# The gated product of a quantised feed-forward block takes its own maximum, and its scale is made before the up projection's

## The reference, cut to what matters

```
def act_qdq(x):
    scale = max(max|x| / 32767, 1e-12)          # one scale for the whole tensor
    return clip(round(x / scale), -32768, 32767) * scale
x    = act_qdq(layernorm(x))
up   = act_qdq(x @ w_up.T)                      # 4096 x 768
gate = act_qdq(x @ w_gate.T)
sig  = round(sigmoid(gate) * 65536) / 65536     # clipped to 65535
gate = act_qdq(gate * sig)
o    = act_qdq(gate * up)
y    = o @ w_down.T
```

## Time and profile before

| | us |
|---|---|
| median of 3 runs (lowest to highest) | 992.13 (990.31 to 997.55) |
| the profiled execution | 989.66 |
| its span in the trace | 987.9 |

### The profile page before, as it was taken

How to read it: one execution, slowest core, us unless ns; L and a number is a source line. 1 busy time by engine, 2 the same in 40 slices (tenths; PEclk the granted TensorE clock), 3 DMA queues, 4 the chain that set the end, 5 groups by cost and what they waited for, 6 DMA issues and landing times.

```text
span 987.9 us, 13059 instructions
## 1 busy us (share of the span) xinstructions
PE 844.3 (85%) x4557; PEld 542.5 (55%) x4559; DVE 680.4 (69%) x1237; ACT 539.2 (55%) x1009; POOL 307.1 (31%) x236
## 2 busy tenths in 40 slices
PE   4999999699999999888998989799998993008998
PEld 3776666578677887344444445344443441005887
DVE  2566777866765677679889999735425999896333
ACT  2444434555234666677667776134329995983342
POOL 2100000566211123588868887200001431000000
PEclk9999999799999999899899999899998997558999
DMA  8800000010000000000000000000002437710111
GB/s 287 267 1 1 1 1 1 0 55 0 2 12 1 1 1 2 1 1 1 1 1 1 2 2 1 0 1 0 1 0 93 163 149 283 263 71 11 54 54 54
DMA packets 23447, 45.43 MB, mean 46 GB/s; under 512 B 2323, under 2 KB 18646, under 8 KB 22230
## 3 DMA queue, kind: packets, MB, share of 16 engines
q1 hardware_dynamic: 21776, 43.08, 12.2%
q10 hardware_dynamic: 1606, 1.52, 0.5%
HBM read 27.80 MB, written 16.78 MB: 45 GB/s over the span
## 4 chain that ended last, share of the span: by engine, by line
PE 62%; DVE 20%; POOL 7%; ACT 5%; issue 4%; DMA 1%; ACTq 1%; DVEq 0%; POOLq 0%
PE pair L1336 8%; PE pair L1290 8%; PE pair L968 5%; PE pair L1206 5%; POOL hat L597 4%; PE pair L1221 3%; PE pair L1076 3%; PE pair L1103 3%; PE pair L972 3%; DVE peak L1784 3%; PE pair L1182 2%; DVE wide L1779 2%; DVE wide L1807 2%; PE pair L1013 2%; DVE peak L1769 2%
## 5 line engine op out<-in xcount | busy, mean ns | idle before, releaser
L597 POOL TENSOR_TENSOR hat<-hat 128x1024 f32<-128x1024 f32 x62 | 145.5, 2362 | 38.2 <-DVE hat L1645 38.1
L1315 PE MATMUL pair<-xqs,wuT 128*128 128x512 f32 x192 | 85.5, 607 | 4.8 <-ACT up_stage L862 4.8
L1290 PE MATMUL pair<-xqs,wgT 128*128 128x512 f32 x192 | 84.3, 596 | 0.0
L1336 PE MATMUL pair<-wdT,hid 128*128 128x256 f32 x384 | 83.1, 379 | 0.4 <-DVE hid L1826 0.4
L1336 PEld LDWEIGHTS pair<-wdT,hid 128*128 128x128 f32 x384 | 72.9, 190 | 11.1 <-DVE hid L1826 1.2
L514 POOL TENSOR_TENSOR rstd<-lnt,half 128x8 f32<-128x8 f32 (+2 forms) x15 | 26.5, 1767 | 168.0 <-DVE lnt L1380 168.0
L1190 PE MATMUL pair<-rows,sel 32*128 32x512 bf16 x256 | 68.3, 396 | 9.9 <-ACT down_a L817 2.9
L1206 PE MATMUL pair<-hat,vz 128*32 128x128 f32 x1056 | 71.6, 282 | 2.8 <-DVE hat L1645 1.6
L1206 PEld LDWEIGHTS pair<-hat,vz 128*32 128x32 f32 x1056 | 53.8, 112 | 25.7 <-issue 23.4
L1315 PEld LDWEIGHTS pair<-xqs,wuT 128*128 128x128 f32 x192 | 37.2, 195 | 52.5 <-issue 52.0
L968 PE MATMUL pair<-wT,ft_sb 128*128 128x256 f32 x256 | 64.6, 396 | 0.0
(11 more groups left out here) (214 smaller groups left out, 1920.7 us busy)
## 6 DMA issues: line engine op xcount, KB each, us to landing
up_far<-up_stage SPq DMA_DIRECT2D x24, 512.0 KB, 2.6
ups<-up_far SPq DMA_DIRECT2D x8, 1536.0 KB, 6.9
x_sb<-in_x_dram SPq DMA_DIRECT2D x8, 512.0 KB, 7.6
c_sb<-in_ctx_dram SPq DMA_DIRECT2D x8, 512.0 KB, 8.6
out_dram<-x_sb SPq DMA_DIRECT2D x16, 256.0 KB, 2.1
four<-in_c_four_dram SPq DMA_DIRECT2D x1, 1280.0 KB, 5.6
deq<-in_L_ffn_w_gate_dram SPq DMA_DIRECT2D x1, 768.0 KB, 7.1
deq<-in_L_ffn_w_up_dram SPq DMA_DIRECT2D x1, 768.0 KB, 8.8
```

Source lines behind the costliest of these rows:

```text
L597: nc.gpsimd.tensor_tensor(hat[:, n % RING, :], hat[:, (n - 2) % RING, :], hat[:, n % RING, :], ALU.add).then_inc(summed, 1)
L1290: last = mm(bank[2 + oc][:], wgT[:, c, oc * 128:(oc + 1) * 128], xqs[:, s, c, :], start=(c == 0), stop=(c == DC - 1))
L1315: last = mm(bank[2 + oc], wuT[:, c, oc * 128:(oc + 1) * 128], xqs[:, t % 2, c, :], start=(c == 0), stop=(c == DC - 1))
L1336: last = mm(bank[s][:, 0:D], hid[:, s, ic, :], wdT[:, ic, :], start=(ic == 0), stop=(ic == IC - 1))
```

## The change

- `gated(h)` becomes one `tensor_tensor_reduce`: it writes the product times -1 into `wide` and the row maximum of what it writes to a column of `peak`. That covers the negative side of the product. `peak_gated` is gone, and the factor that rounds the product (`unit[:, 3, 3:4]`) is made negative, so that the sign comes back.
- The positive side comes from the gate's signed maximum. `peak_gate` takes a maximum and a minimum for each of the first seven quads in place of one absolute maximum; for the last quad the absolute maximum stays ahead of unit 1 and a signed maximum follows behind it. ACT takes the one value per partition through rounding, sigmoid and rounding (`top_sigmoid`, after half 4), DVE multiplies it (`top_product`, at half 8).
- `whole_sigmoid` of the even halves goes from ACT to DVE, h % 4 = 1 from DVE to POOL, h % 4 = 3 from POOL to DVE.
- Units 2 and 3 change places. PE's `spread_peak(2)` stands ahead of the last up pair and serves unit 3. The last three up pairs are copied by ACT behind the last sigmoid; DVE takes two of their maxima between the steps of unit 3, and the third behind it.
- ACT rounds two halves of the gated product ahead of unit 2, and then alternates `whole_up(h)` and `whole_g2(h + 2)`.
- `g2q` takes the first place in the shared memory, `ups` follows; quad t uses slot 1, 0, 2 in turn. SP fetches the first quad of `up_far` once the last gated product is done, ahead of the stores of the last three pairs.

```
@@ -406,7 +408,7 @@
...
         def sig_engine(h):
-            return (0, 1, 0, 2)[h % 4]
+            return (0, 1, 0, 0)[h % 4]
...
@@ -420,7 +422,11 @@
...
         def ups_before(h):
-            return range(3 * h // 2, 3 * (h + 1) // 2)
+            return range((UPS - 3) * h // HALVES, (UPS - 3) * (h + 1) // HALVES)
+        def up_slot(t):
+            return (1, 0, 2)[t % 3]
...
@@ -487,15 +493,20 @@
...
                 sp.wait_ge(up_kept, p + 1)
                 sp.dma_start(up_far[:, p // 3, 2 * (p % 3):2 * (p % 3) + 2, :], up_stage[:, p % 3]).then_inc(up_stored[p % 3], 16)
+                if p == UPS - 4:
+                    for j in range(3):
+                        sp.wait_ge(up_stored[j], 16)
+                    sp.wait_ge(g2_done, HALVES)
+                    sp.dma_start(ups[:, up_slot(0)], up_far[:, 0]).then_inc(up_back[0], 16)
             sp.wait_ge(hid_mm, 2 * NQ * IC)
-            for t in range(NQ):
+            for t in range(1, NQ):
                 for j in range(3):
-                    sp.wait_ge(up_stored[j], 16 * (t + 1))
+                    sp.wait_ge(up_stored[j], 16 * (NQ if t == 2 else t + 1))
                 if t == 2:
-                    sp.wait_ge(g2_done, HALVES)
+                    sp.wait_ge(up_peak, UPS)
                 if t >= 3:
                     sp.wait_ge(up_whole, 2 * (t - 2))
-                sp.dma_start(ups[:, t % 3], up_far[:, t]).then_inc(up_back[t % 3], 16)
+                sp.dma_start(ups[:, up_slot(t)], up_far[:, t]).then_inc(up_back[t % 3], 16)
             sp.wait_ge(x3_done, 2 * NQ)
...
@@ -630,12 +641,12 @@
...
                 sig_free(pool, h)
-                nc.gpsimd.tensor_scalar(sq[:, h % 2], gate_half(h), 65536.0, None, ALU.mult).then_inc(sig_whole[2], 1)
+                nc.gpsimd.tensor_scalar(sq[:, h % 2], gate_half(h), 65536.0, None, ALU.mult).then_inc(sig_whole[1], 1)
...
                 widen(t, t, NQ)
             for h in range(HALVES):
-                if sig_engine(h) == 2:
+                if sig_engine(h) == 1:
                     whole_sigmoid(h)
...
@@ -870,12 +881,18 @@
...
                 act.wait_ge(gate_whole, h + 1)
+                if h == HALVES - 2:
+                    act.wait_ge(hid_peak, 2 * NQ + 1)
                 nc.scalar.activation(gate_half(h), gq[:, h % 4], ACT.Sigmoid, scale=unit[:, 1, 2:3]).then_inc(sig_done, 1)
-            def whole_sigmoid(h):
-                sig_free(act, h)
-                nc.scalar.activation(sq[:, h % 2], gate_half(h), ACT.Copy, scale=65536.0).then_inc(sig_whole[0], 1)
+            def top_sigmoid():
+                act.wait_ge(top_found, 1)
+                nc.scalar.activation(top_i[:, 0:1], peak[:, 1, 2 * NQ:2 * NQ + 1], ACT.Copy, scale=unit[:, 1, 3:4]).then_inc(top_whole, 1)
+                act.wait_ge(top_whole, 1)
+                nc.scalar.activation(top_f[:], top_i[:, 0:1], ACT.Sigmoid, scale=unit[:, 1, 2:3]).then_inc(top_sig, 1)
+                act.wait_ge(top_sig, 1)
+                nc.scalar.activation(top_u[:, 0:1], top_f[:], ACT.Copy, scale=65536.0).then_inc(top_sig, 1)
...
@@ -885,8 +902,10 @@
...
                 for p in ups_before(h):
                     keep_up(p)
-                if sig_engine(h) == 0:
-                    whole_sigmoid(h)
+                if h == 4:
+                    top_sigmoid()
+            for p in range(UPS - 3, UPS):
+                keep_up(p)
...
@@ -895,7 +914,7 @@
...
                 if h >= 4:
                     act.wait_ge(o_done, h - 3)
-                nc.scalar.activation(upq[:, h % 4], ups[:, t % 3, :, h % 2 * 256:(h % 2 + 1) * 256], ACT.Copy, scale=unit[:, 2, 3:4]).then_inc(up_whole, 1)
+                nc.scalar.activation(upq[:, h % 4], ups[:, up_slot(t), :, h % 2 * 256:(h % 2 + 1) * 256], ACT.Copy, scale=unit[:, 2, 3:4]).then_inc(up_whole, 1)
...
@@ -904,16 +923,14 @@
...
             act.wait_ge(unit_step, 1 + 3 * 5)
-            act.wait_ge(g2_done, HALVES)
-            whole_up(0)
-            whole_up(1)
-            for j in range(3):
-                act.wait_ge(up_stored[j], 16 * NQ)
+            act.wait_ge(xqs_ready, 2 * NQ)
+            whole_g2(0)
+            whole_g2(1)
             act.wait_ge(unit_step, 1 + 4 * 5)
             for h in range(HALVES):
-                whole_g2(h)
+                whole_up(h)
                 if h + 2 < HALVES:
-                    whole_up(h + 2)
+                    whole_g2(h + 2)
...
@@ -1267,7 +1284,7 @@
...
                 pe.wait_ge(peak_col, n + 1)
-                nc.tensor.transpose(bank[0][:, 0:128], unit[:, n, 0:1].broadcast_to([128, 128]), IDN).then_inc(peak_spread, 1)
+                nc.tensor.transpose(bank[0][:, 0:128], unit[:, (0, 1, 3, 2, 4)[n], 0:1].broadcast_to([128, 128]), IDN).then_inc(peak_spread, 1)
...
@@ -1319,8 +1336,9 @@
...
                     pe.wait_ge(xq_kept, B)
                     spread_peak(1)
+                if p == UPS - 1:
+                    spread_peak(2)
                 up_pair(p)
-            spread_peak(2)
             spread_peak(3)
...
@@ -1684,6 +1702,7 @@
...
+            V.memset(peak[:, 1, NQ - 1:NQ], 0.0).then_inc(hid_peak, 1)
             V.memset(unit[:, 5:8, :], 1.0).then_inc(unit_step, 1)
...
@@ -1699,26 +1718,37 @@
...
             V.tensor_reduce(peak[:, 0, 0:1], ends[:], AX.XY, ALU.max, apply_absolute_value=True).then_inc(ends_done, 1)
-            def make_unit(n, count):
-                V.tensor_reduce(unit[:, n, 0:1], peak[:, n, 0:count], AX.X, ALU.max).then_inc(peak_col, 1)
-                dve.wait_ge(peak_spread, n + 1)
+            def peak_up(p):
+                dve.wait_ge(up_kept, p + 1)
+                V.tensor_reduce(peak[:, 2, p:p + 1], up_stage[:, p % 3], AX.XY, ALU.max, apply_absolute_value=True).then_inc(up_peak, 1)
+            def make_unit(n, count, between=()):
+                seq = (0, 1, 3, 2, 4)[n]
+                V.tensor_reduce(unit[:, n, 0:1], peak[:, n, 0:count], AX.X, ALU.max, apply_absolute_value=True).then_inc(peak_col, 1)
+                for p in between:
+                    peak_up(p)
+                dve.wait_ge(peak_spread, seq + 1)
                 V.tensor_reduce(unit[:, n, 1:2], bank[0][:, 0:128], AX.X, ALU.max).then_inc(peak_all, 1)
-                dve.wait_ge(peak_all, n + 1)
+                dve.wait_ge(peak_all, seq + 1)
                 raw = unit[:, 5, n:n + 1]
-                k = n * 5 + 1
+                k = seq * 5 + 1
                 V.tensor_tensor(unit[:, n, 4:5], unit[:, n, 1:2], raw, ALU.mult).then_inc(unit_step, 1)
...
                 V.reciprocal(unit[:, n, 5:6], unit[:, n, 2:3]).then_inc(unit_step, 1)
                 dve.wait_ge(unit_step, k + 3)
-                V.tensor_tensor(unit[:, n, 3:4], unit[:, n, 5:6], raw, ALU.mult).then_inc(unit_step, 1)
+                if n == 3:
+                    V.scalar_tensor_tensor(unit[:, n, 3:4], unit[:, n, 5:6], -1.0, raw, ALU.mult, ALU.mult).then_inc(unit_step, 1)
+                else:
+                    V.tensor_tensor(unit[:, n, 3:4], unit[:, n, 5:6], raw, ALU.mult).then_inc(unit_step, 1)
                 if n == 0:
...
                 elif n == 1:
                     V.tensor_scalar(unit[:, 5, 3:4], unit[:, 1, 2:3], 1.0 / 65536, None, ALU.mult).then_inc(unit_step, 1)
-                elif n == 3:
+                elif n == 2:
                     V.tensor_tensor(unit[:, 5, 4:5], unit[:, 3, 2:3], unit[:, 2, 2:3], ALU.mult).then_inc(unit_step, 1)
...
@@ -1742,7 +1772,11 @@
...
             def peak_gate(t):
                 dve.wait_ge(hid_kept, (t + 1) * IC)
-                V.tensor_reduce(peak[:, 1, at(t)], wide[:, :, at_tokens(t)], AX.XY, ALU.max, apply_absolute_value=True).then_inc(hid_peak, 1)
+                if t == NQ - 1:
+                    V.tensor_reduce(peak[:, 1, NQ + t:NQ + t + 1], wide[:, :, at_tokens(t)], AX.XY, ALU.max, apply_absolute_value=True).then_inc(hid_peak, 1)
+                else:
+                    V.tensor_reduce(peak[:, 1, t:t + 1], wide[:, :, at_tokens(t)], AX.XY, ALU.max).then_inc(hid_peak, 1)
+                    V.tensor_reduce(peak[:, 1, NQ + t:NQ + t + 1], wide[:, :, at_tokens(t)], AX.XY, ALU.min).then_inc(hid_peak, 1)
...
@@ -1760,45 +1794,45 @@
...
             by_quad(dve, peak_quad)
             peak_gate(NQ - 1)
-            dve.wait_ge(hid_peak, NQ)
-            make_unit(1, NQ)
-            def peak_up(p):
-                dve.wait_ge(up_kept, p + 1)
-                V.tensor_reduce(peak[:, 2, p:p + 1], up_stage[:, p % 3], AX.XY, ALU.max, apply_absolute_value=True).then_inc(up_peak, 1)
+            dve.wait_ge(hid_peak, 2 * NQ)
+            make_unit(1, 2 * NQ)
+            V.tensor_reduce(peak[:, 1, NQ - 1:NQ], wide[:, :, at_tokens(NQ - 1)], AX.XY, ALU.max).then_inc(hid_peak, 1)
+            dve.wait_ge(hid_peak, 2 * NQ + 1)
+            V.tensor_reduce(peak[:, 1, 2 * NQ:2 * NQ + 1], peak[:, 1, 0:NQ], AX.X, ALU.max).then_inc(top_found, 1)
...
                 sig_free(dve, h)
```

(33 more changed lines are left out.)

## The result

The changed kernel takes 981.06 us (median of 4, 979.25 to 981.46) against 992.05 for the kernel before. The ratio is 0.9883, 95% interval 0.9852 to 0.9913: 11 us, or 1.2%, faster. The forecast was 977.5 in a range of 974 to 987.

What follows compares the result with a forecast made beforehand. DVE was taken to bound the kernel, PE second, 11 us below. The first hidden product 13.5 us earlier gave 976.2 from the profiled 989.66 and 978.6 from the median; forecast 977.5, range 974 to 987.

Steps and rivals of the forecast that it cites:

- The bound and the fusion: Gated phase: DVE loses 26.6 us of reductions, gains 7.0 of roundings; fused product 1.76 us, last one ending at 820.1.
- The halving: Fused DVE product at half throughput, two passes, 3.34 us: some 997.5 to 1000 us in all, chance 0.08.
- The gate phase: Seven second reductions of 3.3 us each hide in DVE's 6.10 us wait for PE's transposes, 2.8 left: no cost.
- the sum: ACT in the gated phase: table, 32 steps of 1.465, 19 up copies and 0.6 us put the end of `sigmoid(15)` at 809.2.
- three small instructions: ACT, gated phase: three added single-column instructions cost 0.6 to 1 us with their waits on each other.
- PE's pace: Up projection: PE restarts at 748.97 and keeps each pair's end, pair 22 at 820.45; after the spread pair 23 ends at 824.3.
- So the product just finds it: POOL's rounding of 4.08 us, asked for 4.2 us or more ahead, is ready when DVE's product needs it.
- Quad 0: Fetch issued at 820.2 lands at 827.1, needed at 828.4: hidden with 1.3 us to spare; at the maximum costs 2.2.
- Quad 1: Fetch issued at 825.6 behind stores, wanted at 834.3: a tie or 1.7 us late; nothing taken for it.
- a wait of `whole_up` for its fetches: Start of the hidden product: if `whole_up` waits for its fetches, the forecast is wrong.
- 13.5 us: Gain up to the first hidden product, which was to start at 830.0 instead of 843.51.
- The point from which the fused product decides: Gated phase: DVE's work of 32.2 + 16d reaches 820 at d = 2.2 us a product, from where it decides the time.

Runs made afterwards that it cites:

- e1: Changed kernel with the plain two-input product in place of the fused instruction and no maximum of the product's negative side: 978.52 us, ratio 0.986.
- e5: Changed kernel with all sixteen roundings of the sigmoid on DVE, none on POOL: 978.85 us, ratio 0.9869.
- e3: Kernel before plus only the fused product, signed maxima and new sharing of the rounding; order of units, copies and fetches as before: 987.86 us, ratio 0.9964.
- e2: Changed kernel's new order alone, with plain product, separate maximum, absolute gate maximum and old sharing of the rounding: 995.69 us, ratio 1.005.
- e6: Changed kernel with an unneeded DVE reduction of 128 x 256 elements behind each fused product: 986.31 us, ratio 0.9937.
- e9: Changed kernel without POOL rounding, quad 1 fetched earlier, pair 20 copied later, pairs 0 and 1 and sigmoid table before unit 1: 973.36 us, ratio 0.9802.
- e4: Changed kernel with POOL rounding halves 3, 6, 9 and 12 in place of 1, 5, 9 and 13: 980.34 us, ratio 0.9875.
- e7: Changed kernel with the fetch of up quad 1 issued ahead of the store of the last up pair: 981.81 us, ratio 0.9909.
- e10: The changed kernel run again, unaltered, against the kernel before: 981.11 us, ratio 0.9856.

## Why the prediction was right

- **The bound and the fusion.** DVE bound the phase, and taking 26.6 us of reductions from it for 7.0 us of rounding put it below PE. The fused product was taken at 1.76 us and its step is 1.68. The halving that a page of the Trainium skill ("Vector Engine (DVE) Microarchitecture Reference", "Points that are easy to get wrong") would have given did not occur in this form of instruction: e1 shows no price at all.
- **The gate phase.** Cover of 6.10 us, 2.8 left, 2.84 measured.
- **ACT and PE.** ACT ended `sigmoid(15)` 69.6 us after unit 1, 2.3 us later than the sum had it, since it waited 2.5 us in all for DVE's products. In e5, with no rounding on POOL, it waited 1.0 us and ended 1.3 us earlier, so a little over half of this was POOL's doing. Its three small instructions took 0.76 us in all, of 0.6 to 1. PE's pace was as forecast.
- **POOL: the step that was mis-sized.** "So the product just finds it" looked at when the rounding would be there, and it was there. It did not look at what DVE's product does while POOL reads. In the kernel before enough work stood ahead of the product to hide it. The DVE instructions of the kernel before that followed the POOL rounding of the earlier trace rows:

```profile
806.28 2.33 DVE L1769 TENSOR_REDUCE peak<-up_stage 128x1 f32<-128x1024 f32 x2
808.53 1.75 DVE L1779 TENSOR_TENSOR wide<-sq,gq 128x1536 f32<-128x1536 uint16 x1
```

The product came 3.67 us after POOL's start at 804.86, behind `peak_gated` and two `peak_up`, and was not stretched. In the changed kernel one `peak_up` stands between, and it comes 0.9 us after. The change took both covers away: the reduction with the fusion, and one of the two `peak_up` with the last three copies moved behind. e3, which loses only the reduction, has no stretched product; e2, which loses only the `peak_up`, has two that take 0.5 us longer. The stalls moved the last product from 78.2 to 79.3, the last up pair from 82.4 to 83.3 and the first hidden product by 1.1 us. e5 takes the roundings off POOL and gets 1.1 us back.
- **The fetches.** Quad 0 was hidden, as forecast. Quad 1 was called a tie or 1.7 us late, priced at nothing, and cost 0.83 us of ACT's time and 0.5 behind it. The prediction named a wait of `whole_up` for its fetches as a sign that it is wrong; that sign appeared, at a price inside the range.
- **The rest.** Of 13.5 us, 1.1 went to POOL's port and 0.5 behind the first hidden product, which leaves 11.9; the medians differ by 11.0. In the profiled pair some 1 us more lies behind the start of unit 4 (90.7 against 89.8 us to the end of the span); its cause is open. The 2.1 us at the start are not the change's.
- **The point from which the fused product decides.** Put at 2.2 us; e6 shows a loss of 3.7 us at 2.0. The sum had DVE's work without POOL's 7.1 us in it, and e6 adds 1.1 us of such stalls to its 5.4 of idle work.

## What to carry to other kernels

When an instruction is taken off the bounding engine, list what stood behind it: it may have been part of the cover for a contention that now shows. Two changes that relieve one path are to be priced together as well as apart. Here, up to the first hidden product, the order alone loses 5 us, the fusion alone brings 6.6 and both bring 12.4; and only both together lay the products open to POOL for long. Then look at what starts the new bound: e9's two copies in an idle stretch brought more than all the repairs at its end.

## What the runs showed of the hardware

- A product on DVE with two 16-bit inputs in SBUF that meets POOL's rounding, already running, waits until 3.07 us after POOL's start, out of 4.08. All 24 such products in the traces of the changed kernel, e1, e2, e4, e6, e7 and e10 start 0.9 to 2.6 us after POOL and end 4.81 to 4.83 us after it; those that start 3.1 us or more after it take 1.75 us (the kernel before, e2, e3). A product of one column waits as long (3.12 us instead of 0.16, e6). In the one case seen, a rounding by `tensor_scalar` on DVE waits for about 4.0 of the 4.08 (e4). `tensor_reduce` isn't stretched in the gated phase of any trace.
- The fused product with maximum costs what the plain one does (2194 against 2201 ns in the mean, stalls included); the instruction that writes the maximum out, 76 ns, hides behind the next.
- After a wait of 9.24 us PE's granted clock was 0.50 (e2), after one of 4.17 us it was 0.58 on average over the next 3 us (e6); the last up pair took 5.91 and 5.29 us instead of 3.60. After 1.22 us it stayed at 1.00 in the changed kernel.
